# Two-layer graph attention on one core: other load order, narrow edge stores and a list of steps spread over more groups in the dense stage

## The reference, cut to what matters

```python
N, E, D, H, C = 12500, 200000, 256, 4, 64        # dst is sorted; edge_attr isn't used
h = maximum(layernorm(x), 0)
def gat_layer(h_in, W, a_s, a_d, b):             # src, dst with one self loop per node appended
    h = (h_in @ W).reshape(n, H, C)
    alpha_s, alpha_d = sum(h * a_s, -1), sum(h * a_d, -1)
    e = leaky_relu(alpha_s[src] + alpha_d[dst], 0.2)
    ex = exp(e - segment_max(e, dst)[dst])
    alpha = ex / segment_sum(ex, dst)[dst]
    return segment_sum(h[src] * alpha[:, :, None], dst).reshape(n, H * C) + b
h = gelu(gat_layer(h, W0, a_src0, a_dst0, b0))   # exact gelu
h = gelu(gat_layer(h, W1, a_src1, a_dst1, b1))
out = x + h
```

## Time and profile before

| | |
|---|---|
| median of 3 runs | 4242.11 us (4241.45 to 4245.93) |
| profiled execution | 4241.65 us, span 4239.8 us |
| GpSimd busy | 3063.3 us, 72% of the span |
| VectorE busy | 3551.8 us, 84% |
| TensorE matmuls | 2746.8 us, 65% |
| ScalarE busy | 2259.7 us, 53% |
| first gather of layer 0 | 181.74 us from the span's start |

### The profile page before, as it was taken

The page is one execution under the profiler, slowest core; times in us unless marked ns, Lnnn a source line. Parts: engine busy times, 40 slices in busy tenths (PEclk is TensorE's granted clock), DMA queues, the critical chain, the costliest instruction groups (busy, mean ns, idle before and its releaser), DMA issues.

```text
span 4239.8 us, 55419 instructions
## 1 busy us (share of the span) xinstructions
PE 2746.8 (65%) x9786; PEld 1883.8 (44%) x9786; DVE 3551.8 (84%) x12391; ACT 2259.7 (53%) x7167; POOL 3063.3 (72%) x3188
## 2 busy tenths in 40 slices
PE   6666666666666666666665666666666666666666
PEld 4444444444444444444443444444444444444444
DVE  5678888888888888888867888888888888888888
ACT  4445555555555555555553555555555555555555
POOL 3277777777777777777747777777777777777774
PEclk9877777777777777777776777777777777777777
DMA  7455555555555555555535555555555555555553
GB/s 215 154 143 151 150 150 151 150 150 150 150 151 150 151 150 150 150 148 149 148 106 145 158 158 158 157 158 158 158 158 157 158 157 155 157 159 157 157 157 102
DMA packets 325448, 645.46 MB, mean 152 GB/s; under 512 B 97250, under 2 KB 194954, under 8 KB 325306
## 3 DMA queue, kind: packets, MB, share of 16 engines
q0 software_dynamic: 151008, 429.04, 37.6%
q1 hardware_dynamic: 128520, 171.76, 13.6%
q10 hardware_dynamic: 45890, 44.36, 3.0%
HBM read 597.18 MB, written 47.71 MB: 152 GB/s over the span
## 4 chain that ended last, share of the span: by engine, by line
POOL 55%; issue 22%; PE 13%; DMA 5%; DVE 3%; ACT 0%; POOLq 0%; DVEq 0%; SPq 0%; ACTq 0%
POOL rows_all L490 55%; PE bank L1086 10%; DMA rows_all<-table,edge 4%; PE bank L1036 1%; PE bank L1094 1%; PE bank L1108 1%; DMA table<-row 1%; DVE stats L738 1%; DVE rows_all L847 0%; DVE ahead L858 0%; PE bank L1073 0%; DMA xg<-in_x_dram 0%; DVE value L852 0%; DVE hnT L760 0%; PE bank L1024 0%
## 5 line engine op out<-in xcount | busy, mean ns | idle before, releaser
L490 POOL DMA_INDIRECT rows_all<-table,edge x3136 | 3023.4, 964 | 1125.0 <-issue 1104.6
L1086 PE MATMUL bank<-rows_all,onehot 128*128 128x264 f32 x6272 | 1872.7, 457 | 19.7 <-DVE rows_all L847 9.9
L1086 PEld LDWEIGHTS bank<-rows_all,onehot 128*128 128x128 f32 x6272 | 1384.1, 228 | 459.5 <-DVE rows_all L847 186.1
L561 ACT ACTIVATE rows_all<-rows_all 128x64 f32<-128x64 f32 x3584 | 878.3, 337 | 3.7
L1068 PE MATMUL bank<-onehotT,logit_p 128*128 128x448 bf16 x896 | 260.5, 423 | 679.0 <-DVE logit_p L838 679.0
L847 DVE TENSOR_TENSOR rows_all<-rows_all,bank 128x768 f32<-128x768 f32 (+1 forms) x672 | 658.8, 1037 | 0.0
L1073 PE MATMUL bank<-ident,ahead 128*4 128x128 f32 x224 | 83.9, 374 | 725.2 <-DVE behind L860 725.2
L573 ACT ACTIVATE share<-node_d 128x8 f32<-128x8 f32 x224 | 46.7, 209 | 872.5 <-DVE node_d L916 872.5
L867 DVE TENSOR_TENSOR onehot<-bank,dloc 128x1792 f32<-128x1792 f32 x224 | 453.5, 2024 | 7.7
L1068 PEld LDWEIGHTS bank<-onehotT,logit_p 128*128 128x128 bf16 x896 | 76.9, 106 | 826.9 <-DVE logit_p L838 770.7
L852 DVE COPY value<-rows_all 128x56 f32<-128x56 f32 x224 | 58.4, 261 | 438.4 <-DMA rows_all<-table,edge 438.4
(11 more groups left out here) (170 smaller groups left out, 3634.8 us busy)
## 6 DMA issues: line engine op xcount, KB each, us to landing
dst_b<-dst_row SPq DMA_DIRECT2D x224, 448.0 KB, 3.9
rows_all<-table,edge POOLq DMA_INDIRECT x3136
self_row<-table SPq DMA_DIRECT2D x224, 132.0 KB
table<-row ACTq DMA_DIRECT2D x113, 132.0 KB
x_row<-in_x_dram SPq DMA_DIRECT2D x112, 128.0 KB, 2.2
out_dram<-y_out ACTq DMA_DIRECT2D x112, 128.0 KB
table<-row ACTq DMA_DIRECT2D x24, 528.0 KB, 3.8
xg<-in_x_dram SPq DMA_DIRECT2D x24, 512.0 KB, 3.6
```

Of the source, the lines that this page charges most:

```text
L490: nc.gpsimd.indirect_dma_start(out=G[u][:, j, :], out_offset=None, in_=table[L][0:N, :], in_offset=bass.IndirectOffsetOnAxis(ap=index[:, j ...
L561: last = nc.scalar.activation(G4[t.u][:, j, h, 0:C], G4[t.u][:, j, h, 0:C], ACT.Copy, scale=G4[t.u][:, j, h, C:C + 1])
L1086: last = nc.tensor.matmul(bank[3 + t.half][:, 0:ROW], onehot[t.half][:, j, :], G[t.u][:, j, :], start=(j == 0), stop=(j == SLOTS - 1))
```

## The change

The loads are issued in another order. SyncE issues W0 first, then two groups of x, then base_i, then the other two groups, and behind them dst, src (which ScalarE issued) and W1. GpSimd sets up its constants ahead of the padding of dst and src. ScalarE runs one Sqrt on the constant eps ahead of everything, and it copies the head columns of layer 0's weights; VectorE is left with the logit columns and no longer waits for W1 and its a. The casts and the matmul that spreads the bases come behind the first group's scales and the first transpose, in bank 0 instead of bank 5, and `find_gaps` reads them. The edge table is stored in 28 pieces of 320 floats of each chunk instead of whole. The list of steps has 16 parts instead of 12 and begins four groups earlier: find_chunks, find_ends and extend_weights(1) are divided. The cut diff:

```diff
+        PIECE = 320
+        PIECES = P * 5 * SLOTS // PIECE
+        STORES = PIECES + 5
+        assert PIECES * PIECE == P * 5 * SLOTS
...
-            for one in from_one:
-                for each in one:
-                    nc.sync.sem_inc(each, 1)
-            for L, W in enumerate((W0, W1)):
-                sp.dma_start(w_in[:, L], W.rearrange("(k p) c -> p k c", p=P)).then_inc(w_landed, 16)
-            sp.dma_start(base_i[0:1, 0:FULL].unsqueeze(2), dst[0:FULL * CH].rearrange("(o c e) -> o c e", o=1, e=CH)[:, :, 0:1],
-                         allow_slow_non_contiguous=True).then_inc(base_landed, 16)
-            sp.dma_start(base_i[0:1, FULL:CHUNKS], dst[FULL * CH:FULL * CH + 1].rearrange("(o c) -> o c", o=1)).then_inc(base_landed, 16)
+            def load_weights(L, W):
+                sp.dma_start(w_in[:, L], W.rearrange("(k p) c -> p k c", p=P)).then_inc(w_landed[L], 16)
...
+            load_weights(0, W0)
+            for one in from_one:
+                for each in one:
+                    nc.sync.sem_inc(each, 1)
             load_group(Group(0, 0))
+            load_group(Group(0, 1))
+            sp.dma_start(base_i[0:1, 0:FULL].unsqueeze(2), dst[0:FULL * CH].rearrange("(o c e) -> o c e", o=1, e=CH)[:, :, 0:1],
+                         allow_slow_non_contiguous=True).then_inc(base_landed, 16)
+            sp.dma_start(base_i[0:1, FULL:CHUNKS], dst[FULL * CH:FULL * CH + 1].rearrange("(o c) -> o c", o=1)).then_inc(base_landed, 16)
+            for j in range(2, XB):
+                load_group(Group(0, j))
+            sp.wait_ge(pad_ready, 3)
             sp.dma_start(dst_c[0:96, :], dst[0:96 * CH].rearrange("(c e) -> c e", e=CH)).then_inc(dst_landed, 16)
-            sp.wait_ge(pad_ready, 3)
             sp.dma_start(dst_c[96:FULL, :], dst[96 * CH:FULL * CH].rearrange("(c e) -> c e", e=CH)).then_inc(dst_landed, 16)
             sp.dma_start(dst_c[FULL:CHUNKS, 0:TAIL], dst[FULL * CH:E].rearrange("(c e) -> c e", c=1)).then_inc(dst_landed, 16)
             sp.dma_start(before_i[1:CHUNKS, :], dst[0:FULL * CH].rearrange("(c e) -> c e", e=CH)[:, CH - 1:CH],
...
-            for j in range(1, XB):
-                load_group(Group(0, j))
+            sp.dma_start(src_c[0:96, :], src[0:96 * CH].rearrange("(c e) -> c e", e=CH)).then_inc(src_landed, 16)
+            sp.dma_start(src_c[96:FULL, :], src[96 * CH:FULL * CH].rearrange("(c e) -> c e", e=CH)).then_inc(src_landed, 16)
+            sp.dma_start(src_c[FULL:CHUNKS, 0:TAIL], src[FULL * CH:E].rearrange("(c e) -> c e", c=1)).then_inc(src_landed, 16)
+            load_weights(1, W1)
...
-            sp.wait_ge(edges_stored, 16 * 6)
+            sp.wait_ge(edges_stored, 16 * STORES)
...
+            link(nc.gpsimd.memset(eps[:], 1e-5))
...
             nc.gpsimd.memset(dst_c[96:CR, :], 1 << 20).then_inc(pad_ready, 1)
             pool.wait_ge(pad_ready, 1)
             nc.gpsimd.memset(src_c[96:CR, :], 0).then_inc(pad_ready, 1)
             pool.wait_ge(pad_ready, 2)
             nc.gpsimd.memset(before_i[:], -1).then_inc(pad_ready, 1)
             pool.wait_ge(pad_ready, 3)
...
-            assert step[0] == CONSTS
...
-            whole = edges_c.rearrange("c p f t -> c (p f t)")
-            for ap, of in ((edges.rearrange("c p w -> c (p w)"), whole), (dst_row, row_c[:]), (marks, marks_c[:].rearrange("c k g -> c (k g)"))):
+            whole, to = edges_c.rearrange("c p f t -> c (p f t)"), edges.rearrange("c p w -> c (p w)")
+            for n in range(PIECES):
+                piece = slice(n * PIECE, (n + 1) * PIECE)
+                pool.dma_start(to[0:CHUNKS, piece], whole[0:CHUNKS, piece]).then_inc(edges_stored, 16)
+            pool.dma_start(to[CHUNKS:CR, :], whole[CHUNKS:CR, :]).then_inc(edges_stored, 16)
+            for ap, of in ((dst_row, row_c[:]), (marks, marks_c[:].rearrange("c k g -> c (k g)"))):
                 pool.dma_start(ap[0:CHUNKS, :], of[0:CHUNKS, :]).then_inc(edges_stored, 16)
                 pool.dma_start(ap[CHUNKS:CR, :], of[CHUNKS:CR, :]).then_inc(edges_stored, 16)
...
-            act.wait_ge(pad_ready, 3)
-            act.dma_start(src_c[0:96, :], src[0:96 * CH].rearrange("(c e) -> c e", e=CH)).then_inc(src_landed, 16)
-            act.dma_start(src_c[96:FULL, :], src[96 * CH:FULL * CH].rearrange("(c e) -> c e", e=CH)).then_inc(src_landed, 16)
-            act.dma_start(src_c[FULL:CHUNKS, 0:TAIL], src[FULL * CH:E].rearrange("(c e) -> c e", c=1)).then_inc(src_landed, 16)
-            act.wait_ge(const_ready, 4)
+                    act.dma_start(a_b[:, L, k, :], a.rearrange("h c -> (h c)").partition_broadcast(P)).then_inc(a_landed[L], 16)
+            act.wait_ge(const_ready, 1)
+            nc.scalar.activation(sdev[0][:, 0:1], eps[:, 0:1], ACT.Sqrt).then_inc(sqrt_begun, 1)
+            act.wait_ge(w_landed[0], 16)
+            for k in range(KC):
+                last = nc.scalar.activation(w_ext[:, 0, k].rearrange("p (h c) -> p h c", h=H)[:, :, 0:C],
+                                            w_in[:, 0, k].rearrange("p (h c) -> p h c", h=H), ACT.Copy)
+            last.then_inc(columns_ready, 1)
+            act.wait_ge(sqrt_begun, 1)
...
+            def logit_columns(L, a):
+                wx = w_ext[:, L].rearrange("p k (h c) -> p k h c", h=H)
+                link(nc.vector.tensor_tensor(w_a[:, a], w_in[:, L], wide(a_b[:, L, a], 1, KC), ALU.mult))
+                return nc.vector.tensor_reduce(wx[:, :, :, C + a], w_a[:, a].rearrange("p k (h c) -> p k h c", h=H), AX.X, ALU.add)
+            def head_columns(L):
                 wx = w_ext[:, L].rearrange("p k (h c) -> p k h c", h=H)
                 for k in range(KC):
                     nc.vector.tensor_copy(wx[:, k, :, 0:C], w_in[:, L, k].rearrange("p (h c) -> p h c", h=H))
...
+            def count_up():
+                dve.wait_ge(const_ready, CONSTS)
+                nc.vector.tensor_copy(iota_f[:], iota_i[:])
+                nc.vector.tensor_copy(node_f[:], node_i[:])
+                nc.vector.tensor_copy(step_no[:], step_no_i[:]).then_inc(cast_ready, 1)
+                dve.wait_ge(base_landed, 32)
+                nc.vector.tensor_copy(base_f[0:1, 1:CHUNKS], base_i[0:1, 1:CHUNKS]).then_inc(base_ready, 1)
...
             def find_gaps():
-                dve.wait_ge(bases_read, 1)
+                dve.wait_ge(bases_done, 1)
                 dve.wait_ge(cast_ready, 1)
+                link(nc.vector.tensor_copy(bases[:], bank[0][:, 0:CR]))
...
                 link(nc.vector.tensor_reduce(chunk_of[:], few, AX.X, ALU.add))
+            def find_places():
                 link(nc.vector.tensor_tensor(pick[:], wide(iota_f[0:hs, 0:CR], 1, 2), wide(chunk_of[:], 2, CR), ALU.is_equal))
                 link(nc.vector.tensor_reduce(inside[:], few, AX.X, ALU.add))
...
                 link(nc.vector.tensor_reduce(until[:], some, AX.X, ALU.add))
+            def find_bases():
                 link(nc.vector.tensor_tensor(picked[:], pick[:], wide(bases[0:hs, :], 1, 2), ALU.mult))
                 link(nc.vector.tensor_reduce(field[:, F_BASE, :], picked[:], AX.X, ALU.add))
...
+            dve.wait_ge(w_landed[0], 16)
+            dve.wait_ge(a_landed[0], 32)
+            for a in range(2):
+                logit_columns(0, a).then_inc(w_ext_ready, 1)
             stats_group(Group(0, 0))
             scales_group(Group(0, 0))
-            LIST = TURNS - 3
+            count_up()
+            LIST = TURNS - 4
...
             between(Group(LIST, 3), Group(LIST, 4))
+            find_places()
+            between(Group(LIST + 1, 0), Group(LIST + 1, 1))
             find_nths()
-            between(Group(LIST + 1, 0), Group(LIST + 1, 1))
+            between(Group(LIST + 1, 1), Group(LIST + 1, 2))
             find_ends()
-            between(Group(LIST + 1, 1), Group(LIST + 1, 2))
+            between(Group(LIST + 1, 2), Group(LIST + 1, 3))
+            find_bases()
+            between(Group(LIST + 1, 3), Group(LIST + 1, 4))
             fill_fields()
-            between(Group(LIST + 1, 2), Group(LIST + 1, 3))
+            between(Group(LIST + 2, 0), Group(LIST + 2, 1))
             count_rounds()
-            between(Group(LIST + 1, 3), Group(LIST + 1, 4))
-            extend_weights(1)
-            between(Group(LIST + 2, 0), Group(LIST + 2, 1))
+            dve.wait_ge(w_landed[1], 16)
+            dve.wait_ge(a_landed[1], 32)
+            between(Group(LIST + 2, 1), Group(LIST + 2, 2))
+            logit_columns(1, 0)
+            between(Group(LIST + 2, 2), Group(LIST + 2, 3))
+            logit_columns(1, 1)
+            between(Group(LIST + 2, 3), Group(LIST + 2, 4))
+            head_columns(1)
+            between(Group(LIST + 3, 0), Group(LIST + 3, 1))
             spread_steps(0)
-            between(Group(LIST + 2, 1), Group(LIST + 2, 2))
+            between(Group(LIST + 3, 1), Group(LIST + 3, 2))
             spread_steps(1)
-            between(Group(LIST + 2, 2), Group(LIST + 2, 3))
+            between(Group(LIST + 3, 2), Group(LIST + 3, 3))
```

(50 more changed lines are left out.)

13 lines of the change are left out of this document (1 added, 12 removed).

## The result

| | before | after |
|---|---|---|
| median of 7 runs | 4242.23 us (4241.22 to 4245.93) | 4227.72 us (4225.9 to 4230.56) |
| profiled execution, span | 4241.65, 4239.8 | 4226.44, 4224.6 |
| first gather | 181.74 | 165.09 |

A forecast was written before the change was run, and what follows sets the result against it. GpSimd's 3136 gathers follow the dense stage, so its gains reach the end in full. Terms -10.0 + 1.2 - 13.2 + 0.4 - 1.8 = -23.4 us gave 4218.7 us, range 4212 to 4227.

The forecast's parts named there:

- start, to the second group: Dense stage's start: earlier loads bring first statistics 8.2 us forward and shorten the next group by 1.8, together -10.0 us.
- shifts behind GpSimd, to the ninth: Groups two to nine: VectorE's shifts wait for GpSimd's edge arithmetic in a whole group more, +1.2 us, bounds -2.3 and +4.
- the store's stall: Edge store in 28 pieces ends ScalarE's wait for a table store, -13.2 us, with +0.4 for later x and stores.
- the list: List of steps in more parts between groups hides more of VectorE's work: -1.8 us, bounds -3 and -1.
- The taking of turns: During the edge store, DMA engines take one packet from each queue in turn; a 1280 B packet takes some 0.07 us.
- 10 us to go: Table stores during the edge store would land in about 6 us, leaving 10 us until their buffer is wanted.
- The 36 us of spreading: The edge store's 14 us of all engines would fit into what x and the table leave, over some 36 us.
- Rival 1: Edge store's stall stays in part, an engine taking a piece's seven rows together: 4222 us, 4231 with stall whole; 9%.
- Rival 2: Start gains 5 us instead of 10, x0 or base_i landing late on the slowest engine: 4223.7 us; 8%.
- rival 3: Gathers wait for the edge store because GpSimd's issues are slow; at 4.5 us each, 4256 us; 2%.
- B: Account from the experiments, not the prediction: the amount standing in GpSimd's queue when a table store comes causes the stall.

The follow-up runs named there:

- e14: Changed kernel with at most four of the 28 pieces of the edge store in flight; 23.5 us faster than the kernel before, ratio 0.9943.
- e18: Kernel before the change, with only the edge store in 28 pieces, four in flight; 4225.09 us, ratio 0.997 to the kernel before.
- e16: Changed kernel with at most four of the 28 pieces in flight, as e14, on another chip; 4213.19 us, ratio 0.9942 to the kernel before.
- e6: Changed kernel with all loads in their old order and GpSimd's fills ahead of its constants; ratio 0.9986 to the kernel before.
- e8: The changed kernel itself, run again beside other experiments; ratio 0.9973 to the kernel before.
- e4: Changed kernel with 7 pieces of 1280 floats, each issued when the one before has landed; ratio 0.9955 to the kernel before.
- e15: Changed kernel with 7 pieces of 1280 floats, two in flight; ratio 0.9961 to the kernel before.
- e1: Changed kernel with the edge table stored whole again, in one piece; ratio 0.998 to the kernel before.
- e12: The changed kernel itself, run again for comparison on one chip; ratio 0.9974 to the kernel before.

## Why the prediction was wrong, point by point

| step | forecast | profile |
|---|---|---|
| start, to the second group | -10.0 | -10.47 |
| shifts behind GpSimd, to the ninth | +1.2 | -0.32 |
| the store's stall | -13.2 + 0.4 | -3.6 |
| the list | -1.8 | -1.95 |
| last statistics to first gather | 0 | -0.3 |
| first gather | -23.4 | -16.65 |

**The step that failed is the one on the store of the edges: "one of 1280 B some 0.07, and the 32 packets of a store or of x take 32 x (0.07 + 0.06 + 0.06) = 6 us".** The taking of turns fits every count, the size of a turn was wrong: 0.15 + 0.05 + 0.05 = 0.25 us, 8 us for the 32. And 8 is not the whole: the store issued at 58.63 moved hardly anything before 64 us, behind the store issued at 53.41 (ScalarE got that one's buffer at 63.20), and then took 12.7 us. Why 12.7 and not 8 stays open: from 64 to 72 us the table's queue moved 518 packets, as many as one store has (512), and yet ScalarE got the buffer only at 76.74; no row tells the 16 engines apart. The margin of "10 us to go" that the step relied on left no room for stores that queue behind one another. My reading of the earlier trace rows had the flaw in sight: 0.15 MB in 48 packets are 3.1 KB each, and I carried over the counts to rows of 1.28 KB as if a packet were always one row. The bytes went, as forecast, into what was left over only where something held them back to it; else the queue takes its turn's worth. The 36 us of spreading came in e14 (pieces issued from 49.55 to 85.17); in the changed kernel the edges were through after some 32 us, and had 61 to 83% of the engines from 58.6 to 74.

Rival 1 named this mechanism (seven rows to a turn) with 9% and priced what is left at 2 to 5 us: 9.65 were left. It let the lag run for 20 us, the time of the issues; in the trace queue 0 kept some 61% or more of the engines until 74 us, and its last packets passed at 82. That this makes up the difference is argued, not shown. The measured time lies between its two prices, 4222 and 4231 with the stall whole. *The rule that stood beside it in the Trainium skill (DMA: Bandwidth & Descriptors, Queues, rings and completion order), an engine drains a packet of several descriptors before it switches, fits the trace, though with 3.0 KB, two to three rows on the mean, and not the 9 to 17 descriptors that it calls typical. With it the forecast would have been 4222 or more.*

The price of the stall itself was right: e18 takes away 13.25 us in the trace and 14.0 in the time. With the stall gone, e14 is at 4217.9 us and the forecast was 4218.7. Some of that closeness is luck: at its first gather (159.03) e14 stands at -22.7, made of -10.3 for the start, +2.9 (not +1.2) for the shifts, -13.2, -1.95 and -0.2; and e16, the same kernel on another chip, is 25.9 us faster than before and not 23.5.

The **start** came out within 0.5 us, term by term (s0 9.20 for 9.3, s0 to s1 4.56 for 4.9), with the weight columns at 8.9 rather than 8.2 still ahead of x. Two numbers on the way to it were off: 2 + 5.1 makes 7.1 for x0 and not 7.5, a slip of 0.4 us inside the allowance of 1.5; and dst landed later than forecast, so that GpSimd's arithmetic began at 20.33 and not near 17.5, and the edges' issues at 49.62 and not 47. The **shift waits** were forecast as +1.2 and measured as -0.3; but the profile of the changed kernel was a lucky one. Its seven groups took 38.5 us; in each of the 15 other profiles with the new load order they took 41.1 to 42.2, +2.2 to +3.4 against before, so the term was too small rather than too large. It hangs on where a shift meets GpSimd's instructions: e14's arithmetic began at the same 20.33, its groups 0.2 us later, and a shift at 22.42 took 2.90 us, until the end of GpSimd's 3.17 us instruction begun at 22.12; the changed kernel's first long one took 1.33, at 27.30. The bounds of -2.3 and +4 held them all. The 2.0 us of such waits that e6 is spared against e8, and the 1.3 us of Sqrt's table that it keeps ahead of x, are in the main why it shows the load order worth 6 and not 10. **Rival 2** and **rival 3** did not come: the 28 issues took 14.63 us, 0.52 each and not 4, and the first gather waited for nothing (`edges_stored` was full at some 82 us).

Open: why 28 unpaced pieces stall by 9.1 in one profile and 12.4 in another; and what the right variable is between 0.57 MB in flight (e4, e14: no stall) and 1.15 MB (e15: 6.7 us). It isn't the number of pieces, four without a stall and two with one, and the rate hardly differs: queue 0 moved 0.82 MB at 66:72 in e4 and 0.81 in e15. That leaves the bytes in flight, which B names, but no run varies them alone.

## What to carry to other kernels

A large store in the background didn't take what was left over here; its queue was served as often as the others, and its rows travelled several to a packet, so cutting it into narrower pieces lowered its share little. Work out what the foreground leaves (here 0.13 MB per us of 0.33) and hold the background down to it, by waiting for an earlier piece before the next is issued: up to 0.57 MB in flight cost nothing, 1.15 MB cost 6.7 us, and GpSimd had nothing else to do. When reading packet counts, divide the bytes by them first.

## What the runs showed of the hardware that I had not expected

Full DMA engines are no sign of trouble by themselves: e4 and e14 held them at 0.89 to 1.05 from 54 to 90 us, and ScalarE waited for no table store.

On the chips of e1 to e12 the gathers' loop itself is slower for every kernel: the same instruction, no longer than elsewhere (954 ns on the mean against 964), has 1884.1 us of idle time before it instead of 1095.8. Of the changed kernel, there (e8):

```profile
L507 POOL DMA_INDIRECT rows_all<-table,edge x3136 | 2991.5, 954 | 1884.1 <-issue 1081.0 <-remote 803.1
```

The 803.1 us are waits that the profile puts down to "remote" and that the changed kernel has not on the other chip; what they are stays open. The dense stage ran as on the other chips, which is why its differences could be measured there.
